# Scatter of both expert layers as row tiles: each product contracts the 64 rows of its batch half

## The chip, the core and the metric

The kernel runs on one core of a Trainium2 chip. A core has five engines that run their own instruction streams and meet at semaphores: PE (TensorE, matrix products into PSUM), DVE (VectorE), ACT (ScalarE), POOL (GpSimd) and SP (SyncE, which issues most transfers here), and 16 DMA engines. The metric is the time of one execution on the device in microseconds (us); less is better.

## What is computed

The input `x` has shape (8, 32, 64, 64): batch, channels, height, width. Four layers are added to it in turn: a spectral convolution (2D Fourier transform, complex product, back), an expert layer on the 4096 tokens of each image, a convolution that sweeps over the image in four directions, row after row, and the same kind of expert layer with other weights. Each layer's input is normalized first. What matters here is the end of an expert layer:

```python
topv = vals.transpose(0, 2, 1)          # the 8 largest gate weights of each expert, over all tokens
topi = idx.transpose(0, 2, 1)           # and which tokens they belong to
...
out = jnp.einsum('ebh,eho->ebo', h, weight2)
out = out.transpose(1, 0, 2)
weighted = jnp.einsum('beo,bke->bkeo', out, topv).reshape(Bn, K * E, O)
outputs = jnp.zeros((Bn, Sn, O), dtype=x.dtype)
outputs = outputs.at[jnp.arange(Bn)[:, None], flat_idx].add(weighted)
```

Each of 16 experts has chosen 8 tokens of each image, and its output vector of 32 channels, times the token's weight, is added to these tokens.

## The kernel before

The image stands in SBUF as 128 rows (4 images x 32 channels) by two halves (images 0 to 3 and 4 to 7: the batch halves `bh`) of 4096 tokens. The scatter is written as a matrix product. `E` has a row for each pair of image and expert (8 x 16 = 128, so rows 0 to 63 belong to batch half 0 and rows 64 to 127 to half 1) and a column for each token; it holds the chosen weights and zero elsewhere. `espread` holds the expert outputs, in 8 blocks of 32 columns, one for each image, and a block is zero in the rows of all other images. The product of 4 blocks (128 columns) with 512 columns of `E` gives the 128 x 512 sums that have to be added to one stretch of 512 tokens of one batch half. So there are 16 products in a layer: 8 stretches (`ch`) for each of 2 halves (`bh`). All values are fp32, and one such product shows in the trace as two passes, each with its own weight load.

**PE** (line 726 on): product `k` goes to PSUM bank `4 + k % 4` and counts up `s_sc`. From product 4 on it waits until the bank is free: for `s_ad`, the count of adds, to reach product k-4's. In layer 0 products 0 to 7 are the stretches of batch half 0 and products 8 to 15 those of half 1; in layer 1 the two halves of a stretch follow each other.

**DVE** waits for `s_sc`, adds the bank to the image in place and counts up `s_ad`: in layer 0 in `add_experts` (line 957) to `RC`, where bank `k` belongs to region `k` of 512 columns, in layer 1 at line 1132 to `RA`.

**Behind layer 0** stands the normalization for the convolution (`norm_tokens(1)`). On PE, `centre_group(1, g)` multiplies 1024 columns of `RC` (regions 2g and 2g+1) with a centring matrix into banks 2(g % 4) and the next. Groups 0 and 1 are woven into the scatter: they are issued behind products 5 and 9 (`FED`). ACT squares a group (line 801) and takes the root of the sums (line 783), DVE sums the squares (`total`, line 934), inverts the root and multiplies (`norm`, lines 941 and 950); then `turn_rows` on PE and copies on ACT (line 790). DVE's own order around the scatter is written out by hand: adds 0 to 5, `total(0)`, adds 6 to 9, `norm(0)`, `total(1)`, adds 10 to 15, `norm(1)`, `total(2)`, and so on. Groups 2 to 7 wait for all 16 adds.

**Behind layer 1** stands only the output: SP waits for two adds at a time (line 379) and issues a store of 512 KB (line 380), eight in all.

Of the kernel before, what the change touches and what calls it, by code (L numbers as in the profile page):

```python
# [10 lines left out]
BL, BH = P // C, B * C // P  # L11
# [7 lines left out]
BANK = 512  # L19
NW = 4  # L20
WRUN = W // NW
MO = P // 2
# [19 lines left out]
def build_kernel(nc, x_in, dft, wspec, conv_w, conv_b, gate_w, gate_b, w1, w2, b2, own, out):  # L42
# [5 lines left out]
    with ExitStack() as ctx:  # L48
        def sb(name, shape, dt=F32):
            return ctx.enter_context(nc.sbuf_tensor(name, shape, dt))  # L50

        def sem(name):
            return ctx.enter_context(nc.semaphore(name))
# [3 lines left out]
        RC, RD = RCD[:, 0:NF], RCD[:, NF:2 * NF]  # L57
        RE = sb("RE", [P, 3 * WCOLS])
        PS = ctx.enter_context(nc.psum_tensor("PS", [P, 8, BANK], F32))
# [21 lines left out]
        espread = sb("espread", [P, B, C])  # L81
# [32 lines left out]
        s_sc, s_ad = sem("scatter_full"), sem("scatter_added")  # L114
# [12 lines left out]
        def blk(region, n):  # L127

            return region[:, n * P:(n + 1) * P]
# [17 lines left out]
        L2, E = RD[:, 0:TOK], RD[:, TOK:2 * TOK]  # L147
# [91 lines left out]
        def ln_slot(g):  # L239

            return banks(2 * (g % 4), 2)
# [189 lines left out]
        def _(pe):  # L431
# [26 lines left out]
            def centre_group(ln, g):  # L458

                if ln == 0:  # L460
                    pe.wait_ge(s_x[g], 16)
                else:
                    pe.wait_ge(s_ad, 2 * g + 2 if g < 2 else 16)
                if g >= 4:
                    pe.wait_ge(s_fd, 8 * ln + g - 3)
                for n in range(8):
                    if ln == 0:
                        m = pe.matmul(blk(ln_slot(g), n), blk(RA, 8 * g + n), centre, start=True, stop=True)  # L468
                    else:
                        first = 1024 * g + BANK * (n // Q)  # L470
                        src = RC[:, first + n % Q:first + BANK:Q]
                        for o in range(0, P, OC):
                            m = pe.matmul(blk(ln_slot(g), n)[o:o + OC], src[:, o:o + OC], centre, start=True, stop=True)  # L473
                m.then_inc(s_cen, 1)

            def norm_tokens(ln, follow):

                def follower(g):
                    pe.wait_ge(s_nrm, 8 * ln + g + 1)
                    follow(g).then_inc(s_ff, 1)  # L480

                if ln == 1:
                    follower(0)
                for g in range(2 * ln, 4):
                    centre_group(ln, g)
                for g in range(ln, 8):
                    follower(g)
                    if 1 <= g < 5:
                        centre_group(ln, g + 3)
# [145 lines left out]
            def experts(l):  # L635
# [8 lines left out]
                for g in range(8):  # L644
# [7 lines left out]
                    for n in range(8):  # L652
                        t, bh = 8 * (g // 2) + n, g % 2
                        src = blk(RC, bh * NT + t) if l == 0 else blk(RA, 8 * g + n)
                        for a in range(2):
                            rows = slice(MO * a, MO * (a + 1))
# [52 lines left out]
                for e in range(NE):  # L709
                    for a in range(2):  # L710
                        units = slice(MO * a, MO * (a + 1))
                        m = pe.matmul(PS[units, 6, B * e:B * e + B], w1_sb[:, e, units], pooled[:, :, e],
                                      start=True, stop=True)
# [11 lines left out]

                pe.wait_ge(s_os, l + 1)
                for k in range(16):
                    if k >= 4:
                        pe.wait_ge(s_ad, 16 * l + k - 3)
                    if l == 0:  # L730
                        bh, ch = divmod(k, 8)
                    else:
                        ch, bh = divmod(k, 2)
                    rhs = E[:, ch * BANK:(ch + 1) * BANK]
                    pe.matmul(PS[:, 4 + k % 4, :], espread[:, BL * bh:BL * bh + BL, :].rearrange("p b o -> p (b o)"), rhs,  # L735
                              start=True, stop=True).then_inc(s_sc, 1)
                    if l == 0 and k in FED:
                        centre_group(1, FED.index(k))

            experts(0)  # L740


# [14 lines left out]
            for s in range(4):  # L757
# [12 lines left out]
                for r in range(1, H):  # L770
                    step(r // Q, r % Q)

            experts(1)


# [148 lines left out]
        def _(dve):  # L924
# [6 lines left out]
            def norm_tokens(ln):  # L931
                def total(g):
                    dve.wait_ge(s_sq, LNS[ln] + g + 1)
                    dve.tensor_reduce(sums[:, 32 * g:32 * g + 32],  # L934
                                      square[:, g % 2, 0:1024].rearrange("p (a c) -> p a c", c=C), AX_X,
                                      ALU.add).then_inc(s_sum, 1)

                def norm(g):
                    r = rstd[:, 32 * g:32 * g + 32]
                    dve.wait_ge(s_std, LN0[ln] + g + 1)  # L940
                    dve.reciprocal(r, std[:, 32 * g:32 * g + 32]).then_inc(s_rec, 1)
                    dve.wait_ge(s_rec, LN0[ln] + g + 1)
                    if ln == 0:
                        m = dve.tensor_tensor(RD[:, 1024 * g:1024 * g + 1024].rearrange("p (a c) -> p a c", c=C),
                                              ln_slot(g).rearrange("p (a c) -> p a c", c=C),
                                              r.unsqueeze(2).to_broadcast([P, 32, C]), ALU.mult)
                    else:
                        for hb in range(2):
                            k = slice(BANK * hb, BANK * (hb + 1))
                            m = dve.tensor_tensor(  # L950
                                RA[:, 1024 * g:1024 * g + 1024][:, k].rearrange("p (b j c) -> p j b c", b=BL, j=Q),
                                ln_slot(g)[:, k].rearrange("p (j b c) -> p j b c", b=BL, j=Q),
                                r[:, 16 * hb:16 * hb + 16].rearrange("p (j b) -> p j b", b=BL).unsqueeze(3)
                                .to_broadcast([P, Q, BL, C]), ALU.mult)
                    m.then_inc(s_nrm, 1)

                def add_experts(first, last):

                    for k in range(first, last):
                        x2 = RC[:, BANK * k:BANK * (k + 1)]  # L960
                        dve.wait_ge(s_sc, k + 1)
                        dve.tensor_tensor(x2, PS[:, 4 + k % 4, :], x2, ALU.add).then_inc(s_ad, 1)

                if ln == 0:
                    total(0)
                    total(1)
                    norm(0)
                    total(2)
                    norm(1)
                    total(3)  # L970
                    norm(2)
                else:
                    add_experts(0, FED[0] + 1)
                    total(0)
                    add_experts(FED[0] + 1, FED[1] + 1)
                    norm(0)
                    total(1)
                    add_experts(FED[1] + 1, 16)
                    norm(1)
                    total(2)  # L980
                    total(3)
                    norm(2)
                for g in range(3, 8):
                    if g < 7:
                        total(g + 1)
                    norm(g)
# [9 lines left out]
            for a in range(2):  # L996
                rows = slice(MO * a, MO * (a + 1))
# [24 lines left out]
            for a in range(2):  # L1022
                rows = slice(MO * a, MO * (a + 1))
# [217 lines left out]
```

## Time and profile before

| | us |
|---|---|
| median of 3 runs | 577.56 |
| the runs | 576.42 to 582.18 |
| the profiled execution | 579.15 |
| its span, from first to last instruction | 577.3 |
| PE busy in the span | 516.2 (89%) |
| DVE, ACT, POOL busy | 323.8, 275.8, 113.3 |
| share of L735 (PE) in the chain that ended last | 5% |

A row of the profile names line, engine, operation and tiles (output<-inputs), then shape and type, then how often (x) and its time. PE stands for the matrix passes, PEld for weight loads. L735 is line 735 of the code. The chain of waits follows the work that ended last, back from the end; a row of it is one stretch of that chain. `RCD` is the tensor of which `RC` and `RD` are the halves, and `RE`, `RA`, `RB` are other large buffers.

### The profile page before, as it was taken

Reading aid. Unit: us, or ns where it says so; the run is one execution under the profiler, and the core shown is the slowest. Engines: PE = TensorE matmul, PEld = TensorE weight load, DVE = VectorE, ACT = ScalarE, POOL = GpSimd, SP = SyncE. Lnnn points to the kernel's source line nnn. Section 1 sums busy time; section 2 is a strip of 40 time slices with the busy share of each in tenths; the row PEclk is TensorE's granted clock in tenths of the full one; section 3 lists DMA queues with packets and bytes.
Section 4 is the critical chain, followed back from the end, with each engine's and each line's share of the span. In section 5 each row is a group of like instructions: output and inputs, shape, how many; then the busy total and the mean of one; then the engine's idle time right before and its main releaser. Section 6 shows DMA issues by size and latency. Waiting matters only on the chain.

```text
span 577.3 us, 25417 instructions
## 1 busy us (share of the span) xinstructions
PE 516.2 (89%) x11282; PEld 462.0 (80%) x11282; DVE 323.8 (56%) x767; ACT 275.8 (48%) x782; POOL 113.3 (20%) x240
## 2 busy tenths in 40 slices
PE   8878999768857999969999999889999999756997
PEld 8878998668747975859999888778899999756973
DVE  2757565833459537754544554445555445669626
ACT  3546554435577102654444444434446777748100
POOL 4000000000161000003333333643331033451000
PEclk9999999989996979988999999979999999976979
DMA  9940990051000000000000033410000244500007
GB/s 351 373 147 2 328 373 36 1 219 76 5 3 1 2 20 2 3 0 3 4 5 3 4 79 76 115 35 4 4 4 3 45 81 82 99 1 1 2 2 291
DMA packets 50259, 41.69 MB, mean 72 GB/s; under 512 B 44998, under 2 KB 45126, under 8 KB 48934
## 3 DMA queue, kind: packets, MB, share of 16 engines
q1 hardware_dynamic: 49304, 38.51, 20.8%
q8 instruction: 90, 1.47, 1.2%
q0 software_dynamic: 704, 1.18, 0.9%
q10 hardware_dynamic: 144, 0.39, 0.2%
q14 instruction: 17, 0.14, 0.1%
HBM read 27.49 MB, written 4.19 MB: 55 GB/s over the span
## 4 chain that ended last, share of the span: by engine, by line
PE 79%; DVE 8%; ACT 6%; POOL 4%; issue 3%; DMA 0%; SPq 0%; POOLq 0%; ACTq 0%; DVEq 0%
PE PS L766 40%; PE PS L550 6%; PE PS L494 5%; PE PS L735 5%; PE PS L591 3%; PE PS L532 3%; PE PS L685 3%; PE PS L473 2%; POOL RE L394 2%; PE PS L436 2%; POOL RCD L397 2%; PE PS L503 2%; DVE sums L1052 1%; PE PS L454 1%; PE PS L468 1%
## 5 line engine op out<-in xcount | busy, mean ns | idle before, releaser
L766 PE MATMUL PS<-RE,conv_sb 128*64 128x64 f32 x6048 | 231.2, 230 | 4.4 <-DVE RE L1151 4.0
L766 PEld LDWEIGHTS PS<-RE,conv_sb 128*64 128x64 f32 x6048 | 210.3, 139 | 25.4 <-DVE RE L1151 4.7
L901 ACT COPY PS<-convb_sb 128x64 f32<-128x64 f32 x504 | 108.2, 215 | 113.0 <-DVE RE L1163 102.6
L1163 DVE SCALAR_TENSOR_TENSOR RE<-PS,RCD 128x64 f32<-128x64 f32 x252 | 56.5, 224 | 58.3 <-PE PS L766 50.0
L406 POOL COPY RCD<-RE 128x128 f32<-128x128 f32 x126 | 37.1, 294 | 156.7 <-DVE RE L1163 156.6
L1163 DVE SCALAR_TENSOR_TENSOR RE<-PS,RE 128x64 f32<-128x64 f32 x126 | 32.6, 259 | 28.4 <-PE PS L766 21.0
L1163 DVE SCALAR_TENSOR_TENSOR RE<-PS,RB 128x64 f32<-128x64 f32 x126 | 28.3, 224 | 28.2 <-PE PS L766 28.2
L494 PE MATMUL PS<-warm 128*128 128x128 bf16 x418 | 35.6, 261 | 3.9 <-DVE warm L929 1.4
L494 PEld LDWEIGHTS PS<-warm 128*128 128x128 bf16 x418 | 32.6, 120 | 5.1 <-ACT RB L879 1.6
L394 POOL TENSOR_TENSOR RE<-RA 128x1024 f32<-128x1024 f32 x3 | 5.7, 1892 | 149.5 <-ACT RA L872 149.5
L550 PE MATMUL PS<-RE,RB 128*64 128x64 f32 x1024 | 32.2, 223 | 1.6 <-DVE RA L991 1.4
L550 PEld LDWEIGHTS PS<-RE,RB 128*64 128x64 f32 x1024 | 30.9, 138 | 2.8 <-issue 2.0
L934 DVE TENSOR_REDUCE sums<-RE 128x32 f32<-128x1024 f32 x16 | 19.4, 1218 | 23.7 <-ACT RE L801 23.7
L1052 DVE TENSOR_REDUCE sums<-RE 128x32 f32<-128x1024 f32 x16 | 19.2, 1201 | 20.7 <-POOL RE L394 17.0
L735 PE MATMUL PS<-RCD,espread 128*128 128x512 f32 x64 | 29.6, 616 | 0.0
L801 ACT ACTIVATE RE<-PS 128x1024 f32<-128x1024 f32 x16 | 16.2, 1022 | 24.1 <-PE PS L473 21.0
L1008 DVE COPY RB<-PS 32x1024 f32<-32x1024 f32 x16 | 19.4, 1214 | 14.7 <-PE PS L532 14.5
L406 POOL COPY RB<-RE 128x128 f32<-128x128 f32 x63 | 18.5, 294 | 40.9 <-DVE RE L1163 40.9
L790 ACT COPY RCD<-PS 128x256 f32<-128x256 f32 (+1 forms) x40 | 17.6, 510 | 15.1 <-PE PS L503 7.7
L591 PE MATMUL PS<-dft_sb,RB 128*128 128x128 f32 x128 | 17.1, 294 | 7.9 <-ACT RE L843 7.6
L735 PEld LDWEIGHTS PS<-RCD,espread 128*128 128x128 f32 x64 | 12.5, 201 | 14.3 <-issue 13.8
L591 PEld LDWEIGHTS PS<-dft_sb,RB 128*128 128x128 f32 x128 | 16.0, 205 | 8.7 <-issue 8.3
(117 smaller groups left out, 691.9 us busy)
## 6 DMA issues: line engine op xcount, KB each, us to landing
RE<-wspec SPq DMA_DIRECT2D x8, 2048.0 KB, 8.7
RA<-x_in SPq DMA_DIRECT2D x8, 512.0 KB, 7.4
RCD<-x_in SPq DMA_DIRECT2D x1, 4096.0 KB, 12.3
out<-RA SPq DMA_DIRECT2D x8, 512.0 KB, 2.7
RCD<-RB SPq DMA_DIRECT2D x58, 64.0 KB, 2.6
RE<-RCD SPq DMA_DIRECT2D x32, 80.0 KB, 2.6
conv_sb<-conv_w SPq DMA_DIRECT2D x1, 768.0 KB, 20.1
w_sb<-w SPq DMA_DIRECT2D x2, 264.0 KB
```

The lines of the kernel that those rows point to most:

```text
L406: pool.tensor_copy(o, i).then_inc(s_arc, 1)
L494: pe.matmul(PS[:, bank, 0:P], warm[:, :], warm[:, :], start=True, stop=True)
L550: m = pe.matmul(o[:, x % 2, y], XB[:, c % 2, 2 * KYC * x + 2 * y + a].rearrange("p r q b -> p (r q b)"), WR[:, c % 3, a, x, y, :], start=T ...
L591: m = pe.matmul(blk(dft_h_slot(g), n), blk(RB, KY * (g % 2) + 8 * (g // 2) + n), inv_h, start=True, stop=True)
L735: pe.matmul(PS[:, 4 + k % 4, :], espread[:, BL * bh:BL * bh + BL, :].rearrange("p b o -> p (b o)"), rhs, start=True, stop=True).then_inc(s ...
L766: m = pe.matmul(conv_bank(s, u, c)[o:o + OC], conv_sb[:, s, d, o:o + OC], prev, start=False, stop=(d == 2), skip_group_check=True)
L790: m = act.copy(o, i)
L901: act.copy(banks_of, convb_sb[:, s:s + 1].unsqueeze(2).to_broadcast([P, c1 - c0, n])).then_inc(s_seed, 1)
L934: dve.tensor_reduce(sums[:, 32 * g:32 * g + 32], square[:, g % 2, 0:1024].rearrange("p (a c) -> p a c", c=C), AX_X, ALU.add).then_inc(s_su ...
L1008: m = dve.tensor_copy(o, i)
L1052: dve.tensor_reduce(sums[:, 32 * g:32 * g + 32], square[:, g % 2, 0:1024].rearrange("p (a c) -> p a c", c=C), AX_X, ALU.add).then_inc(s_su ...
L1163: dve.scalar_tensor_tensor(out=state[:, state_slot(s, u), b0:b1, 1:1 + HO], in0=conv_bank(s, u, c), scalar=0.0, in1=row_at(SRC[s], s, q, u ...
```

## The change

Every product now takes only the 64 rows of its own batch half, of `espread` and of `E` alike; the other 64 rows of `espread` were zero there. In both layers products 2j and 2j+1 are the two batch halves of the same 512-token stretch j, so they use different rows of the array and neighbouring banks. The wait for free banks is taken by the even product for both. In layer 0 the order of the stretches is new, so `add_experts` computes the region, and the first two centre groups wait for other counts: group 0 for 3 adds in place of 2 (products 0 and 2 hold its regions), group 1 for 7 in place of 4 (products 4 and 6).

```diff
@@ centre_group
-                    pe.wait_ge(s_ad, 2 * g + 2 if g < 2 else 16)
+                    pe.wait_ge(s_ad, 4 * g + 3 if g < 2 else 16)
@@ experts, on PE
                 pe.wait_ge(s_os, l + 1)
                 for k in range(16):
-                    if k >= 4:
-                        pe.wait_ge(s_ad, 16 * l + k - 3)
-                    if l == 0:
-                        bh, ch = divmod(k, 8)
-                    else:
-                        ch, bh = divmod(k, 2)
-                    rhs = E[:, ch * BANK:(ch + 1) * BANK]
-                    pe.matmul(PS[:, 4 + k % 4, :], espread[:, BL * bh:BL * bh + BL, :].rearrange("p b o -> p (b o)"), rhs,
-                              start=True, stop=True).then_inc(s_sc, 1)
+                    if k >= 4 and k % 2 == 0:
+                        pe.wait_ge(s_ad, 16 * l + k - 2)
+                    ch, bh = divmod(k, 2)
+                    rows = slice(MO * bh, MO * (bh + 1))
+                    pe.matmul(PS[:, 4 + k % 4, :], espread[rows, BL * bh:BL * bh + BL, :].rearrange("p b o -> p (b o)"),
+                              E[rows, ch * BANK:(ch + 1) * BANK], start=True, stop=True).then_inc(s_sc, 1)
                     if l == 0 and k in FED:
                         centre_group(1, FED.index(k))
@@ add_experts, on DVE
-                        x2 = RC[:, BANK * k:BANK * (k + 1)]
+                        region = 8 * (k % 2) + k // 2
+                        x2 = RC[:, BANK * region:BANK * (region + 1)]
```

The order of instructions on every engine stays; what moves is where PE waits. This is PE in layer 0 from the last warming products to centre group 0 (L473): first before, then after, a line number lower by three (`scatter_added` is `s_ad`, `experts_spread` is `s_os`).

```order
-L735 MATMUL PS<-RCD,espread 128x512 [waits experts_spread]
-L735 MATMUL PS<-RCD,espread 128x512 x3
-L735 MATMUL PS<-RCD,espread 128x512 [waits scatter_added] x2
+L732 MATMUL PS<-RCD,espread 128x512 [waits experts_spread]
+L732 MATMUL PS<-RCD,espread 128x512 x3
+L732 MATMUL PS<-RCD,espread 128x512 [waits scatter_added]
+L732 MATMUL PS<-RCD,espread 128x512
 L473 MATMUL PS<-dft_sb,RCD 64x128 [waits scatter_added]
```

Products 4 and 5 each waited; now product 4 waits for both and product 5 follows without a wait. The same goes for the pairs behind the centre groups. This is PE at the end of the program, layer 1's scatter, before:

```order
L735 MATMUL PS<-RCD,espread 128x512 [waits experts_spread]
L735 MATMUL PS<-RCD,espread 128x512 x3
L735 MATMUL PS<-RCD,espread 128x512 [waits scatter_added] x12
L48 UNCONDITIONAL_BRANCH
```

There every product from the fifth on waited for an add of its own; after the change every second one does, in six pairs like that of layer 0.

## Rows read from the trace of the kernel before

**Rows 1.** The span, and all instructions of L735: duration in ns, least, median, most.

```profile
core 0 of [0], span 577.3 us
L735 PEld LDWEIGHTS PS<-RCD,espread x64: 186/190/337, 211.1 to 572.4; 128*128 128x128 f32 x64
L735 PE MATMUL PS<-RCD,espread x64: 592/592/1167, 211.2 to 572.8; 128*128 128x512 f32 x64
```

**Rows 2.** The chain of waits in order of time: start, us, engine, tile, line, count.

```profile
135.07 1.16 PE PS L454 x64
136.23 0.64 PE PS L436 x16
...
211.44 5.57 PE PS L735 x12
...
231.10 4.06 PE PS L473 x64
...
558.88 14.53 PE PS L735 x32
573.43 0.69 DVE RA L1136
```

**Rows 3.** Timeline of layer 0's scatter: start, us, engine, line, operation [idle before, releaser].

```profile
212.76 0.69 DVE L962 TENSOR_TENSOR RCD<-PS,RCD 128x512 f32<-128x512 f32 x1 [1.97 <-PE PS L735]
...
216.94 2.19 PE L473 MATMUL PS<-dft_sb,RCD 128*64 128x128 f32 x32
...
219.18 1.02 ACT L801 ACTIVATE RE<-PS 128x1024 f32<-128x1024 f32 x1 [12.58 <-PE PS L473]
...
220.24 1.22 DVE L934 TENSOR_REDUCE sums<-RE 128x32 f32<-128x1024 f32 x1 [2.49 <-ACT RE L801]
...
221.37 2.48 DVE L962 TENSOR_TENSOR RCD<-PS,RCD 128x512 f32<-128x512 f32 x4
...
222.69 2.19 PE L473 MATMUL PS<-dft_sb,RCD 128*64 128x128 f32 x32
223.76 0.34 DVE L941 RECIPROCAL rstd<-std 128x32 f32<-128x32 f32 x1
224.14 1.29 DVE L950 TENSOR_TENSOR RA<-PS,rstd 128x512 f32<-128x512 f32 x2
...
225.98 1.22 DVE L934 TENSOR_REDUCE sums<-RE 128x32 f32<-128x1024 f32 x1 [0.55 <-ACT RE L801]
...
227.12 3.84 DVE L962 TENSOR_TENSOR RCD<-PS,RCD 128x512 f32<-128x512 f32 x6
...
231.03 1.16 PEld L473 LDWEIGHTS PS<-dft_sb,RCD 128*64 128x64 f32 x18 [0.17 <-DVE RCD L962]
```

**Rows 4.** Busy time by stretch (us): PE, PEld, DVE, ACT, POOL, PE clock, DMA share, GB/s.

```profile
133.50:151.00 17.50, 14.97 (x647) 13.50 (x642) 9.26 (x8) 8.50 (x9) 0.00 (x0) 1.00 0.02 5
211.20:212.05 0.85, 0.85 (x4) 0.48 (x2) 0.00 (x0) 0.00 (x0) 0.00 (x0) 0.50 0.00 0
558.60:560.20 1.60, 1.60 (x5) 0.85 (x4) 0.00 (x0) 0.00 (x0) 0.00 (x0) 0.50 0.00 0
```

**Rows 5.** Timeline of layer 1's scatter.

```profile
560.55 0.69 DVE L1136 TENSOR_TENSOR RA<-PS,RA 128x512 f32<-128x512 f32 x1 [2.33 <-PE PS L735]
...
561.41 0.69 DVE L1136 TENSOR_TENSOR RA<-PS,RA 128x512 f32<-128x512 f32 x1 [0.17 <-PE PS L735]
...
562.13 12.39 SPq L380 DMA_DIRECT2D out<-RA  x8
```

**Rows 6.** Stretches of the stores: ahead of the first, inside it, behind the last.

```profile
562.50:563.00 0.50, 0.50 (x3) 0.26 (x2) 0.46 (x1) 0.00 (x0) 0.00 (x0) 1.00 0.00 0
563.50:564.00 0.50, 0.50 (x3) 0.24 (x2) 0.33 (x2) 0.00 (x0) 0.00 (x0) 1.00 1.01 385
576.50:577.30 0.80, 0.00 (x0) 0.00 (x0) 0.00 (x0) 0.00 (x0) 0.00 (x0) 0.98 0.00 0
```

## The prediction

> **What bounds the kernel now.** I read the page first, then the chain of waits in order of time, then the timeline of the two stretches that the diff touches, then windows for the TensorE clock and the DMA engines. PE is busy through most of the span, but the scatter (L735) is a small part of it: its 64 passes (32 products, two passes each) [rows 1] stand in two places. In the chain, layer 0's scatter and the two centre groups woven into it begin at 211.44 and the two centre groups behind it at 231.10; layer 1's scatter runs from 558.88 for 14.53 us, and behind it stand one add and the last store [rows 2]. So of 577.3 us some 34 can move at all.
>
> In both places PE sets the pace. In layer 1 the adds of 0.69 us begin 0.86 us apart, as the products come, and DVE idles between them [rows 5]. 0.86 us is two passes of 0.43. DVE can do better: the four adds at 221.37 had their products waiting and took 2.48 us in all, which, with 0.69 for one, is (2.48 - 0.69) / 3 = 0.60 us from one start to the next [rows 3].
>
> **The change part by part.** One: a product of 128 rows becomes one of 64, and both batch halves of a stretch follow each other, on different rows of the array and into different banks. Nothing is removed: 32 products of 512 columns stay. The gain depends on both halves streaming at once. No row shows this for 512 columns, so I bound it. If they stream together, a pair costs what one product costs now, 0.86 us; if not, 1.72. The nearest rows are L454 and L436. L454 makes 64 passes of 64 columns in 1.16 us [rows 2]; at L735's 0.43 us for 512 columns these would take 64 x 0.43 / 8 = 3.44 one by one, so three stream at once, on a quarter of the array each. With only two at once (one row half, both column halves) they would need 1.72. L436 is cut as the new products are (64 rows, all 128 columns of the array): 16 passes in 0.64 us [rows 2] where one by one they need 0.86. I take full overlap, 0.86 a pair, since a 512-column pass has its 0.19 us weight load [rows 1] behind it.
>
> Two: the wait. Before, product k waited for add k-4. Now the even product waits for both adds of the pair before last, and the odd one rides with it. A wait costs: 0.07 us from an add's end (227.12 + 3.84 = 230.96) to the next load (231.03) [rows 3], about 0.1 of the load that no stream covers, 0.43 for the first pass, 0.59 for the whole of the second [rows 1], 0.03 to the add: 1.22 us from add to add. Two banks are being added meanwhile, 1.20 us. So PE and DVE come out almost even: a pair begins 0.60 + 0.69 + 1.22 = 2.51 after the pair before last, 1.26 us a pair against 1.72 now. Queued behind the waiting product on PE are the centre groups in layer 0 and nothing in layer 1.
>
> **Layer 0, step by step** [rows 3]. The first products stream at half clock until 212.05 [rows 4], before and after alike, so add 0 stays at 212.76; adds 1 to 3 follow 0.60 apart. Add 1 ends at 213.36 + 0.69 = 214.05. Products 4 and 5 are streamed by 214.05 + 0.07 + 0.1 + 0.86 = 215.08, and centre group 0 begins at about 215.17 in place of 216.94: 1.77 early. Adds 4 and 5 end at 216.57, ahead of its square. The square (219.18), the sum (220.24) and the adds behind it (221.37) therefore come 1.77 early, so add 6 begins at 219.60. Products 6 to 9 are there by then.
>
> Centre group 1 now waits for add 6, not add 3, since the order of the regions is new. Add 6 ends at 219.60 + 0.69 = 220.29, PE is idle from about 219.1, and the group begins at 220.36 in place of 222.69. This idle costs nothing: its square ends when DVE has done adds 6 to 9 and the norm (223.76 - 1.77, then 0.34 and 1.29), near 223.65. The 0.55 us that DVE now waits ahead of its sum at 225.98 goes too. So that sum comes 2.33 early, add 10 begins near 224.8, products 14 and 15 wait for add 11 and cost DVE 0.1, and add 15 ends at 228.58 in place of 230.96. Centre group 2 waits for all 16 adds before and after, the rest is a chain of PE, ACT and DVE, and layer 0 gives **2.4 us**.
>
> **Layer 1** [rows 5, 6]. Add 0 stays at 560.55. With 1.26 us a pair the last add ends at 560.55 + 7 x 1.26 + 1.29 = 570.7 in place of 573.43 + 0.69 = 574.12, which would be 3.4 us. But each pair of adds releases a store of 512 KB. Today a store moves at 385 GB/s, all 16 DMA engines busy (share 1.01), 1.36 us each, within the 1.72 us of a pair, so each is over before the next. With pairs every 1.26 us the stores queue. The first is issued at 560.55 + 0.60 + 0.69 = 561.84 instead of 562.13, its packets begin 0.9 to 1.0 later (now 563.0), and eight of them take 10.9 us: to 573.7. Now the last packets are over by 576.5, so the end comes **2.7 us** sooner and DMA paces the end. The adds have 0.8 us to spare there.
>
> The Trainium skill, in "TensorEngine Tiling (Array Packing)", section PSUM Bottleneck, says that tiling speeds up TensorE and not the emptying of PSUM, which may become the limit. By that rule the adds would end layer 1: 3.4 us there and 5.8 in all. The stores' share of 1.01 speaks for one limit further on; no row shows eight stores back to back.
>
> **Sum.** 2.4 + 2.7 = 5.1 us off the profiled execution's 579.15, whose span is 577.3: 574.1. The median of the three runs, 577.56, lies 1.6 lower, so I forecast 577.56 - 5.1 = **572.5**. A difference of about 1% (5.8 us) is what a measurement of this kernel can tell from no change, and the runs shown spread from 576.42 to 582.18.
>
> **The rivals.** *The pair overlaps in part.* L454's passes took 1.16 where four at once would take 0.86; at that ratio a pair costs 1.16, 0.3 more. Layer 0 pays it at the first pair, at products 4 and 5 and at 14 and 15 (0.9), layer 1 at the first pair and 0.05 a pair (0.6): 574.0. The Trainium skill, in "TensorE: Matmul & The Clock Gate", Part 3, gives 3.07 times for four row tiles of 512 columns, the same ratio as L454's.
>
> *The adds, not the stores, end layer 1.* For it: stores that follow each other could hide their start. Against it: share 1.01. It gives 571.8.
>
> *The clock falls.* PE would stream 0.86 of every 1.26 us, and stand still for 1.2 us ahead of centre group 1 and near 2 ahead of product 14. The clock was at its lower level as both scatters began [rows 4], after sparse work. If it fell again, the two centre groups behind the scatter, 4.06 us at the full clock [rows 2], would pay up to 4; I take 2.5: 575. Against it: the stretch with 64-row tiles from 133.5 was at 1.00 throughout [rows 4].
>
> *No overlap at all.* The pair takes 1.72, PE sets the pace as now, and the waits bind nowhere: 577.5. The change would then do nothing. Against it: L454 and L436.
>
> *Slower: the halves shut each other out.* If the array had to empty before the other half's rows load and stream, each product would cost 0.1 + 0.43 + 0.59 = 1.12 us in place of 0.86, which is 16 x 0.26 = 4.2 us a layer, 8.4 in all: 586. It decides against the change from a pair of more than 1.72 us on. Against it: L436 alternates between the row halves and gains.
>
> **How the numbers follow.** Forecast 0.60, adds 0.07, part overlap 0.12, clock 0.08, no overlap 0.07, shut out 0.06. The forecast alone would lie within 570.5 to 574.5, the spread of the runs taken in. The range goes from 569.5 (the adds' 571.8, less the 1.1 by which the fastest run lies under the median, less about 1 for a scatter that meets the low clock for less long) to 577.0, just under no change; that leaves out the last two rivals and some of the clock's, under 2 in 10. Faster by over 1% means under 571.8: 0.38 of the forecast, half of the adds', a little of part overlap: 0.28, and I say 0.29. Slower is the last rival: 0.06. Same: 0.65.
>
> **What would show it.** In layer 1: adds in pairs 0.6 apart, pairs 1.26 apart; the last add over near 570.7; DMA share near 1.0 from 563 to the end. In layer 0: centre group 0 some 1.8 us and group 2 some 2.4 us earlier after the scatter's start; PE idle about 1.2 us ahead of centre group 1. Wrong if products of one pair end 0.86 apart (no overlap), if adds spaced further than 1.36 us a pair end layer 1, if DVE's add grows beyond 0.69 while two halves stream, or if the granted clock is below 1.00 between the scatter's second pair and centre group 3.

## The result, and the profile after

Before: median 579.3 us (4 runs, 576.42 to 582.18). Changed: median **570.9 us** (4 runs, 568.43 to 573.18). The ratio is 0.9895 with a 95% interval of 0.9845 to 0.9944, so 6.1 us less, with 3.2 to 9.0 in the interval. It leaves out two runs of before that count as slow (582.18 and 581.04), so the two medians lie further apart than it says. In a second, longer comparison (below) it was 0.9941 (0.9909 to 0.9972), 3.4 us less. The forecast was 5.1 us and 572.5.

The profiled executions differ by more: 577.3 us of span before and 566.6 after. Part of that is not the change's, so the two scatters are read by themselves. First the timeline of layer 0's scatter in the changed kernel (start, us, engine, line, operation, then idle time before and what ended it); the line numbers are lower by two or three.

```profile
206.81 0.48 DVE L1125 SCALAR_TENSOR_TENSOR espread<-PS,rsum,own_sb 128x256 f32<-128x256 f32 x1 [0.85 <-PE PS L722]
207.88 4.58 PE L732 MATMUL PS<-RCD,espread 64*128 64x512 f32 x12
209.99 3.79 DVE L960 TENSOR_TENSOR RCD<-PS,RCD 128x512 f32<-128x512 f32 x6 [2.70 <-PE PS L732]
...
212.39 2.19 PE L473 MATMUL PS<-dft_sb,RCD 128*64 128x128 f32 x32
...
214.51 1.99 PE L732 MATMUL PS<-RCD,espread 64*128 64x512 f32 x8
214.62 1.02 ACT L798 ACTIVATE RE<-PS 128x1024 f32<-128x1024 f32 x1 [11.06 <-PE PS L473]
...
215.68 1.22 DVE L931 TENSOR_REDUCE sums<-RE 128x32 f32<-128x1024 f32 x1 [1.90 <-ACT RE L798]
216.82 2.48 DVE L960 TENSOR_TENSOR RCD<-PS,RCD 128x512 f32<-128x512 f32 x4
...
217.55 2.19 PE L473 MATMUL PS<-dft_sb,RCD 128*64 128x128 f32 x32 [1.06 <-DVE RCD L960]
...
220.84 1.22 DVE L931 TENSOR_REDUCE sums<-RE 128x32 f32<-128x1024 f32 x1
221.98 3.78 DVE L960 TENSOR_TENSOR RCD<-PS,RCD 128x512 f32<-128x512 f32 x6
...
225.81 4.11 PE L473 MATMUL PS<-dft_sb,RCD 128*64 128x128 f32 x64 [0.35 <-DVE RCD L960]
```

Counted from the first add (209.99; before 212.76 [rows 3]), centre group 0 begins after 2.40 us (before 4.18), group 1 after 7.56 (before 9.93), and the last add is over after 221.98 + 3.78 - 209.99 = 15.77 (before 18.20). The first six adds stand in one row of 3.79 us: DVE no longer idles between them. PE idles 1.06 us ahead of group 1.

The row at 214.51 is products 6 to 9, two pairs: eight passes in 1.99 us. First products 6 to 9 in the kernel before, with two of their weight loads, then two of the weight loads in the row at 214.51. The loads are 0.43 us apart in both, one by one before and in twos now:

```profile
219.06 3.70 PE L735 MATMUL PS<-RCD,espread 128*128 128x512 f32 x8
219.60 0.19 PEld L735 LDWEIGHTS PS<-RCD,espread 128*128 128x128 f32 x1 [0.24 <-issue]
220.03 0.19 PEld L735 LDWEIGHTS PS<-RCD,espread 128*128 128x128 f32 x1 [0.24 <-issue]
```

```profile
215.04 0.19 PEld L732 LDWEIGHTS PS<-RCD,espread 64*128 64x128 f32 x2 [0.23 <-issue]
215.47 0.19 PEld L732 LDWEIGHTS PS<-RCD,espread 64*128 64x128 f32 x2 [0.24 <-issue]
```

The lead holds behind the scatter. From the first add to the first product of the convolution (L766, then L763) it is 258.94 - 212.76 = 46.18 us before and 253.91 - 209.99 = 43.92 changed, 2.3 less:

```profile
258.94 5.25 PE L766 MATMUL PS<-RE,conv_sb 128*64 128x64 f32 x108 [0.40 <-ACT PS L901]
```

```profile
253.91 5.36 PE L763 MATMUL PS<-RE,conv_sb 128*64 128x64 f32 x110 [0.40 <-ACT PS L898]
```

Layer 1's scatter:

```profile
549.33 0.48 DVE L1125 SCALAR_TENSOR_TENSOR espread<-PS,rsum,own_sb 128x256 f32<-128x256 f32 x1 [0.60 <-PE PS L722]
...
552.33 10.00 DVE L1134 TENSOR_TENSOR RA<-PS,RA 128x512 f32<-128x512 f32 x16 [2.51 <-PE PS L732]
553.64 9.08 SPq L380 DMA_DIRECT2D out<-RA  x8
```

The sixteen adds take 10.0 us in place of 13.57. The chain of waits (start, us, engine, tile, line, count) now changes sides with every pair, PE and DVE about even, where before it was 14.53 us of PE [rows 2]; it ends with the last add, so the stores behind that show in the windows further down and not here:

```profile
553.67 1.18 PE PS L732 x4
554.85 1.28 DVE RA L1134 x2
556.17 1.18 PE PS L732 x4
557.35 1.28 DVE RA L1134 x2
```

Windows (busy time of PE, PEld, DVE, ACT, POOL, then the granted clock of PE, the DMA share and GB/s): the start of layer 0's scatter and the rest of it, then the stores.

```profile
207.88:210.65 2.77, 2.77 (x9) 1.18 (x8) 0.66 (x2) 0.00 (x0) 0.00 (x0) 0.50 0.00 0
210.65:225.80 15.15, 11.99 (x100) 6.83 (x96) 13.20 (x22) 4.27 (x7) 0.00 (x0) 1.00 0.01 2
...
554.50:565.50 11.00, 5.94 (x22) 1.50 (x20) 7.76 (x13) 0.00 (x0) 0.00 (x0) 1.00 1.01 376
565.90:566.60 0.70, 0.00 (x0) 0.00 (x0) 0.00 (x0) 0.00 (x0) 0.00 (x0) 0.50 0.00 0
```

The DMA engines are full (1.01) from the first store to the end, where one store had been over before the next [rows 6]. From layer 1's first add to the end of the span: 14.27 us, before 16.75.

So the two scatters give 2.4 and 2.5 us from their first add on. The rest of the 10.7 us lies elsewhere, cut at the end of `espread` and of the last add: 3.5 ahead of layer 0's scatter, 3.2 between the two, and in each layer from `espread` to the first add something given back (0.7 and 0.2), which the experiments come to.

### The profile page after: what moved, and what is told of

It is laid out like the page before. It is cut to its first block, busy times and chain, and to the rows that moved or that the text cites. A ratio compares the mean times of both kernels' runs of the same rounds, so it can differ in the third digit from the quotient of the medians.

```text
span 566.6 us, 25417 instructions
## 1 busy us (share of the span) xinstructions
PE 498.5 (88%) x11282; PEld 450.4 (79%) x11282; DVE 321.6 (57%) x767; ACT 275.7 (49%) x782; POOL 115.1 (20%) x240
## 4 chain that ended last, share of the span: by engine, by line
PE 73%; DVE 13%; ACT 6%; POOL 4%; issue 2%; DMA 0%; DVEq 0%; SPq 0%; POOLq 0%; ACTq 0%
PE PS L763 41%; PE PS L550 6%; PE PS L494 4%; PE PS L532 3%; PE PS L591 3%; PE PS L685 3%; POOL RCD L397 2%; POOL RE L394 2%; PE PS L436 2%; PE PS L473 2%; PE PS L732 2%; PE PS L503 2%; DVE sums L931 2%; DVE sums L1050 2%; PE PS L454 1%
## 5 line engine op out<-in xcount | busy, mean ns | idle before, releaser
L763 PE MATMUL PS<-RE,conv_sb 128*64 128x64 f32 x6048 | 231.3, 231 | 4.5 <-DVE RE L1149 4.1
L763 PEld LDWEIGHTS PS<-RE,conv_sb 128*64 128x64 f32 x6048 | 212.7, 139 | 23.0 <-DVE RE L1149 4.8
L494 PE MATMUL PS<-warm 128*128 128x128 bf16 x418 | 31.1, 241 | 3.9 <-DVE warm L926 1.4
L494 PEld LDWEIGHTS PS<-warm 128*128 128x128 bf16 x418 | 28.4, 109 | 4.9 <-ACT RCD L876 1.6
L591 PE MATMUL PS<-dft_sb,RB 128*128 128x128 f32 x128 | 15.7, 279 | 7.9 <-ACT RE L840 7.6
L732 PE MATMUL PS<-RCD,espread 64*128 64x512 f32 x64 | 19.1, 699 | 2.8 <-DVE RCD L960 1.7
L591 PEld LDWEIGHTS PS<-dft_sb,RB 128*128 128x128 f32 x128 | 14.7, 192 | 8.6 <-issue 8.2
L659 PE MATMUL PS<-proj,RA 64*64 64x96 f32 x512 | 14.1, 273 | 8.0 <-DVE RA L343 4.4
```

Source lines behind the costliest of these rows:

```text
L494: pe.matmul(PS[:, bank, 0:P], warm[:, :], warm[:, :], start=True, stop=True)
L591: m = pe.matmul(blk(dft_h_slot(g), n), blk(RB, KY * (g % 2) + 8 * (g // 2) + n), inv_h, start=True, stop=True)
L732: pe.matmul(PS[:, 4 + k % 4, :], espread[rows, BL * bh:BL * bh + BL, :].rearrange("p b o -> p (b o)"), E[rows, ch * BANK:(ch + 1) * BANK], ...
L763: m = pe.matmul(conv_bank(s, u, c)[o:o + OC], conv_sb[:, s, d, o:o + OC], prev, start=False, stop=(d == 2), skip_group_check=True)
```

## The experiments

**How much is the change's: both kernels again.** Nothing edited.

> The changed kernel again, nothing edited, timed in more rounds. Theory A (the two scatters give about 5 us, the rest of the 10.7 us between the two profiled spans is the TensorE clock's lower level met for longer or shorter): from the first add to the end of the last add of layer 0 again 15.8 us (before 18.2), from layer 1's first add to the end of the span again 14.3 us (before 16.75), each within 0.2; the stretch between the two scatters (last add of layer 0 to the end of espread in layer 1, 327.3 before and 324.1 after) may come out anywhere from 323 to 329; the ratio to before near 0.991. Theory B (the change does more than the scatters): that stretch between stays at 324, and the ratio lies near 0.985.

> The kernel before again, nothing edited, for a second trace. Theory A (the stretches without the change differ from run to run with the clock): 18.2 us and 16.75 us in the two scatter stretches again, within 0.2 each, while the stretch between the scatters may come out from 323 to 329 in place of 327.3, and goes with the time spent at the lower clock: about half of any difference in it. Theory B: it stays at 327.3 within 0.5.

Measured: 572.84 us (12 runs) against 577.31 (17 runs), ratio 0.9941 (0.9909 to 0.9972); the second trace of before is one run of 578.02. The scatter stretches repeat: changed 15.93 and 14.22 us, before 18.20 and 16.74. The stretch between the scatters does not belong to either kernel. Its windows, for before, for changed, and for two kernels of the experiments below, the one with 128 rows back and the one with half stores:

```profile
230.96:558.22 327.26, 302.63 (x7410) 276.00 (x7409) 178.12 (x584) 168.85 (x651) 93.73 (x225) 0.95 0.15 29
```

```profile
225.76:549.81 324.05, 299.69 (x7408) 275.94 (x7409) 177.47 (x584) 168.59 (x651) 95.56 (x225) 0.96 0.15 29
```

```profile
232.96:555.80 322.84, 297.84 (x7410) 262.23 (x7409) 178.27 (x585) 168.91 (x651) 93.92 (x225) 0.97 0.15 29
```

```profile
227.99:550.81 322.82, 298.21 (x7408) 262.57 (x7409) 178.25 (x584) 168.67 (x651) 94.15 (x225) 0.97 0.15 29
```

In these four the length goes with the granted clock, 0.95, 0.96, 0.97, 0.97, and not with the scatter: the third one has 128-row products and no gain there, and yet is as short as the fourth. Over all eleven traces clock and length go together only roughly (the second trace of "halves in a row", below, has 327.0 us at 0.95 and "its own wait" 325.4 at 0.96, where changed has 324.1 at 0.96), so that the clock is all of it is not shown. The stretch lay between 322.8 and 327.6; before came out at 327.3 and 327.6, changed at 324.1 and 324.8, with the edits below at 322.8 to 327.0. The two traces of each kernel fit theory B as well as A; it is the edited kernels, short with 128 rows (322.8) and long with 64 (326.7 with a store behind each add), that speak for A. The stretch ahead of layer 0's scatter was 210.8 and 209.0 us in before, 207.3 and 210.3 in changed. So the 6.7 of the 10.7 us that lie in these two stretches come and go with the execution.

**128 rows back in each product.**

```diff
-                    rows = slice(MO * bh, MO * (bh + 1))
+                    rows = slice(0, P)
```

> The changed kernel with the 128 rows back in each product; order of the stretches, the waits for pairs and for the centre groups stay as changed. Theory A (the gain is that two row halves stream at once): two products of 128 rows cannot, so a pair takes 1.72 us, the adds come 0.86 apart, and the stretches are those of before: 18.2 us in layer 0 and 16.75 us in layer 1, within 0.4. Theory B (the new order and the waits bring the gain): 15.8 and 14.3 stay.

Measured: 577.09 us (one run). Layer 0 18.41 us, layer 1 16.97. The adds of layer 1 are 0.86 apart again (timeline):

```profile
559.40 0.69 DVE L1134 TENSOR_TENSOR RA<-PS,RA 128x512 f32<-128x512 f32 x1 [0.39 <-PE PS L732]
560.25 0.69 DVE L1134 TENSOR_TENSOR RA<-PS,RA 128x512 f32<-128x512 f32 x1 [0.17 <-PE PS L732]
561.11 0.69 DVE L1134 TENSOR_TENSOR RA<-PS,RA 128x512 f32<-128x512 f32 x1 [0.17 <-PE PS L732]
```

With the order and the waits of the change and without its rows the gain is gone; both stretches are those of before within 0.25 us. That is theory A.

**64 rows, but the halves in a row.** Layer 0 in the order, waits and regions of before, layer 1 as changed.

```diff
-                    pe.wait_ge(s_ad, 4 * g + 3 if g < 2 else 16)
+                    pe.wait_ge(s_ad, 2 * g + 2 if g < 2 else 16)
...
-                    if k >= 4 and k % 2 == 0:
-                        pe.wait_ge(s_ad, 16 * l + k - 2)
-                    ch, bh = divmod(k, 2)
+                    if k >= 4 and (l == 0 or k % 2 == 0):
+                        pe.wait_ge(s_ad, 16 * l + k - (3 if l == 0 else 2))
+                    if l == 0:
+                        bh, ch = divmod(k, 8)
+                    else:
+                        ch, bh = divmod(k, 2)
...
-                        region = 8 * (k % 2) + k // 2
+                        region = k
```

> The changed kernel with layer 0's products back in the order, the waits and the regions of before (all eight of batch half 0, then all eight of half 1), each still of 64 rows; layer 1 stays as changed. Theory A (a product of 64 rows costs what one of 128 rows costs, and only neighbours on different rows stream at once): layer 0 as before, products 0.86 apart and 18.2 us, but for the two in the middle where the half changes; layer 1 14.3. Theory B (a product of 64 rows is cheaper by itself): layer 0 well under 18.2, near 15.8.

Measured: 581.48 us (one run), layer 0 **23.12 us**, layer 1 14.25. Neither theory had that. On PE (timeline, then windows):

```profile
211.70 10.61 PE L735 MATMUL PS<-RCD,espread 64*128 64x512 f32 x12
222.24 3.70 PE L473 MATMUL PS<-dft_sb,RCD 128*64 128x128 f32 x32
225.86 2.63 PE L735 MATMUL PS<-RCD,espread 64*128 64x512 f32 x8
...
230.53 5.45 PE L735 MATMUL PS<-RCD,espread 64*128 64x512 f32 x12
```

```profile
211.70:222.20 10.50, 10.50 (x13) 3.84 (x12) 3.46 (x5) 0.00 (x0) 0.00 (x0) 0.50 0.00 0
222.20:227.18 4.98, 4.98 (x37) 4.11 (x38) 0.84 (x2) 1.18 (x2) 0.00 (x0) 0.50 0.01 3
227.18:237.00 9.82, 9.82 (x60) 5.18 (x58) 9.79 (x16) 2.79 (x4) 0.00 (x0) 1.00 0.00 1
```

PE streams without a pause, and still the clock stays at 0.50 (1.2 GHz) from the first product to 227.18, 15.5 us; the kernel before reached 1.00 (2.4 GHz) 0.8 us after its first product [rows 4]. At the lower clock the first adds come 1.71 us apart, one product each. At the full clock the last six products cost 0.86 each (5.45 for 12 passes), like products of 128 rows [rows 5]. So theory A holds for the price of a product, and the clock is a second cost that was not in it. The clock rose 1.3 us into the row at 225.86, four products of both halves behind centre group 0; which of the two lifted it no run separates.

**The same again, and with four full products ahead.** The second kernel differs from "halves in a row" in one line:

```diff
-                    rows = slice(MO * bh, MO * (bh + 1))
+                    rows = slice(0, P) if l == 0 and k < 4 else slice(MO * bh, MO * (bh + 1))
```

> The kernel with layer 0's products of 64 rows in the order of before, again, to see whether the clock's long stay at its lower level was chance. In the first run of it the clock stayed at 0.50 from the first product for 15.5 us, through ten products one by one and centre group 0, where the kernel before rose 0.8 us after its first product. Theory A (64-row products one at a time do not lift the clock): again at 0.50 through the first six products and the centre group, first add to last add 22 us or more. Theory B (chance): the clock rises within about 4 us of the first product and the stretch is 18.2 to 19.5.

> The same kernel, but with 128 rows in layer 0's first four products; products 4 to 15 keep 64 rows, one after another. Theory A: the four full products lift the clock as in the kernel before, within about 2 us of the first; two 64-row products and a centre group follow, which is too little to bring it down, so the stretch is that of before, 18.2 to 18.5 us, and products of 64 rows take 0.86 us at the full clock. Theory B (64-row products also let the clock fall): the clock is at 0.50 again somewhere before the last add, and the stretch is over 19.5.

Measured, one run of each: the first again 23.12 us, at 0.50 until 228.16, 15.5 us again (583.91). With four full products the clock rose 1.9 us after the first, stayed at 1.00, and the stretch was 17.59 us (572.55). A window of the first, two of the second, then the timeline of the second:

```profile
212.68:228.16 15.48, 15.48 (x49) 7.95 (x50) 4.30 (x7) 1.19 (x2) 0.00 (x0) 0.50 0.01 1
```

```profile
207.54:209.46 1.92, 1.92 (x5) 0.89 (x4) 0.00 (x0) 0.00 (x0) 0.00 (x0) 0.50 0.00 0
209.46:227.18 17.72, 17.32 (x103) 9.20 (x101) 14.01 (x22) 3.97 (x5) 0.00 (x0) 1.00 0.01 1
```

```profile
207.54 6.52 PE L735 MATMUL PS<-RCD,espread 128*128 128x512 f32 x12
...
216.11 1.99 PE L735 MATMUL PS<-RCD,espread 64*128 64x512 f32 x8
...
220.15 3.70 PE L735 MATMUL PS<-RCD,espread 64*128 64x512 f32 x8
```

Both rows of x8 are four products: 220.15 those of one half, one by one, 3.70 us; 216.11 two of either half, 1.99. The second is the likely reason why the stretch is under the 18.2 expected. Both runs give theory A, but for that.

**Half of each store left out.**

```diff
-                sp.dma_start(halves[:, i // 2, i % 2], done[:, i // 2, i % 2]).then_inc(s_out, 16)
+                sp.dma_start(halves[:, i // 2, i % 2, 0:1], done[:, i // 2, i % 2, 0:1]).then_inc(s_out, 16)
```

> The changed kernel with half of each store left out: only batch half 0 of each pair of adds is written to the output, 256 KB in place of 512 KB, so half of the output is missing. Everything ahead of it stays. Theory A (the stores that queue end layer 1): they do not queue any more, and the end follows the last add at the distance of one short store: the adds take 10.0 us as now, and the end comes about 2.5 us behind them, 12.5 us from the first add in place of 14.27. Theory B (the adds and a fixed tail end it): the tail stays near 4.3 less the 0.7 of the shorter last store, 13.6 us.

Measured: 567.73 us (one run). The adds take 9.99 us as ever, the end comes 12.43 us behind the first add (14.27 changed), 2.44 behind the last (4.27). The windows of the stores:

```profile
555.50:565.00 9.50, 6.11 (x24) 1.50 (x20) 7.92 (x13) 0.00 (x0) 0.00 (x0) 0.94 0.58 220
```

At a share of 0.58 nothing queues, and the adds end the layer. Of the 1.8 us some 0.7 is the shorter last store; the rest, 1.1, is the queue; by as much the changed kernel ends further behind its last add than the kernel before (4.27 against 3.19). That is theory A.

**A store behind each add; group 2 waits for 14 adds.**

```diff
-                    pe.wait_ge(s_ad, 4 * g + 3 if g < 2 else 16)
+                    pe.wait_ge(s_ad, (3, 7, 14)[g] if g < 3 else 16)
...
-            for i in range(2 * NW):
+            for i in range(4 * NW):
...
-                sp.wait_ge(s_ad, 16 + 2 * (i + 1))
-                sp.dma_start(halves[:, i // 2, i % 2], done[:, i // 2, i % 2]).then_inc(s_out, 16)
+                k, h, t = i // 4, i // 2 % 2, i % 2
+                sp.wait_ge(s_ad, 16 + i + 1)
+                sp.dma_start(halves[:, k, h, t], done[:, k, h, t]).then_inc(s_out, 16)
```

> The changed kernel with two further edits. Layer 1: a store of 256 KB behind each add in place of 512 KB behind two, sixteen stores. Layer 0: centre group 2 waits for 14 adds in place of 16 (its banks and regions are free by then). Theory A (the queue of stores ends layer 1 and begins with the first store; layer 0's end hangs on centre group 2): the first store begins one add, 0.6 us, earlier and the end with it: 13.7 us from layer 1's first add in place of 14.27; centre group 2 begins 0.6 us earlier, 15.2 us behind layer 0's first add in place of 15.82. Together 1.2 us, too little for the whole time to tell. Theory B (each store has a cost of its own on the queue): sixteen stores end later than eight, 14.5 us or more.

Measured: 569.19 us (4 runs, 567.72 to 570.28), ratio to before 0.9859 (0.9784 to 0.9934). The end of layer 1 comes 13.47 us behind the first add (0.8 sooner than changed), centre group 2 begins 15.41 us behind layer 0's first (0.4 sooner; not 0.6, since PE is busy with the follower until then). The queue, over 11 us:

```profile
556.50:567.50 11.00, 6.63 (x24) 1.66 (x24) 8.45 (x14) 0.00 (x0) 0.00 (x0) 1.00 1.02 378
```

It is as full as with eight stores, only earlier. That is theory A. By its stretches this version is 1.2 us ahead of the changed kernel, and in layer 0 the lead holds to the first product of the convolution (43.33 us from the first add, 43.92 changed). So it is the best one here; the whole times don't tell the two apart.

**Each product its own wait.**

```diff
-                    if k >= 4 and k % 2 == 0:
-                        pe.wait_ge(s_ad, 16 * l + k - 2)
+                    if k >= 4:
+                        pe.wait_ge(s_ad, 16 * l + k - 3)
```

> The changed kernel with the waits of before: from product 4 on each product waits for the add four ahead of it, the odd ones too, in place of one wait for the pair. Rows, order and regions stay as changed. Theory A (what sets the adds' pace is the way round from an add to the add that its bank allows, 1.2 us plus an add): with a way round of 4 adds in place of two pairs the adds come 0.60 apart all through, 9.7 us from the first add's start to the last add's end in layer 1 in place of 10.0; the end of the span does not move, since the stores end it: 14.25 from the first add. Layer 0 15.5 to 15.8 as now. Theory B (the two halves stream together only where the odd product rides with the even one): products come one by one, 0.86 apart, and layer 1 goes back to 13.6 and 16.75.

Measured: 569.3 us (one run). Layer 1's adds in one row (timeline), and 14.26 us to the end:

```profile
553.24 9.74 DVE L1134 TENSOR_TENSOR RA<-PS,RA 128x512 f32<-128x512 f32 x16 [2.70 <-PE PS L732]
```

Layer 0 15.66 us. The common wait is not what lets the halves overlap; it costs 0.26 us in layer 1, behind which the stores stand anyway. That is theory A.

## Why the prediction was right, step by step

- **The pair streams in the time of one product: right.** At the full clock the passes of both halves start within 0.01 us of each other, and the next two 0.43 later (0.53 behind the first passes of a row); 128-row products in the same places bring nothing. The part-overlap rival is out for 512 columns, no overlap and shut-out too.
- **The way round, 1.26 us a pair: right.** Measured 10.0 us for 16 adds, so (10.0 - 1.29) / 7 = 1.24. With own waits it is DVE's 0.60 an add alone.
- **Layer 0, 2.4 us: right from the first add on.** Group 0 came 1.78 us sooner (forecast 1.77), group 1 2.37 (2.33), the last add's end 2.43 (2.38), 2.27 in the second pair of traces; PE's idle ahead of group 1 was 1.06 (1.2) and cost nothing.
- **"Before and after alike" for the start: wrong.** From the end of `espread` to layer 0's first add it took 1.97 and 2.36 us in before and 2.70 in both traces of changed: 0.3 to 0.7 us given back. The first pass starts 0.59 us behind `espread` in place of 0.45, and the whole first pair and most of the second meet the lower clock (207.88 to 210.65 at 0.50), which in before rose during the first product. Not all of that is the change's: with 128 rows in the first products and the clock low through the first one (four full products ahead) it took 2.51. So about 0.2 us goes with the 64 rows, and whether the change also makes the clock rise later is open: it rose 0.8 to 2.3 us after the first pass with 128 rows and 1.5 to 4.0 with pairs, both layers taken together. Layer 1 gave back about 0.2 (2.33 and 2.37, then 2.51 and 2.56).
- **Layer 1, 2.7 us, the stores end it: right in mechanism, 0.2 too large.** The eight stores took 11.3 us (packets from 554.58 to 565.84), not 10.9 (the forecast's own figures, 576.5 less 573.7, make 2.8). The adds' rival, 3.4 us for layer 1, falls by the 1.1 us that the queue adds. The Trainium skill's rule in "TensorEngine Tiling (Array Packing)", section PSUM Bottleneck, that the emptying of PSUM may become the limit, fits the pace of the adds with own waits (9.74 us in one row) and not the end of the layer.
- **The clock's rival: not in the change, but near it.** In the first trace of changed the clock was at 1.00 from the end of the second pair (210.65) to the end of the scatter, pauses and all; in the second trace it rose 3.8 us after the first pass, DVE idled 0.42 us between its first two pairs, and the stretch was 15.93 us. Products that stream one half alone are where it stayed low; there it had not risen, and it did not fall once up.
- **Sum: right, 0.7 to 1.2 us too large; the total is in part luck.** 2.43 + 2.48, less 0.5 to 1.0 at the two starts, is 3.9 to 4.4 us where 5.1 were forecast; both measured ratios hold it in their intervals. Taken off 577.56 that gives 573.2 to 573.7, and the twelve runs gave 572.84. The median of 570.9 is lower, and the stretches that the change doesn't touch, which the profiled run had short, lie on that side.

## What to carry to other kernels

Products that contract only half of the rows are free to pair: put neighbours on different rows (and, as here, in different banks; no run varied the banks) and the pair costs one product. Then look for what paces the stretch next, twice over; here it was the adds with PE in one place and the output queue in the other, and of the 6.9 us a layer that pairing takes off PE (8 x 0.86) 2.4 and 2.5 were left. Where two profiles differ by more than the stretches that were changed, read the granted clock of the rest before the change is given credit for it.

## What the hardware did that was not expected

**Half the rows, one product at a time, left the clock low.** Two traces, the same both times: 15.5 us of unbroken streaming at 0.50 (six such products, centre group 0 and a part of the next four), where 128 rows in the same order were at 1.00 after 0.8 and 1.6 us in the two traces of before. With pairs of halves the clock rose 1.6 to 3.8 us after their first pass, in five traces. Once up, the clock stayed up over 3.70 and 5.45 us of single halves.

**Products on other rows overtake.** In the kernel with the halves in a row, products 6 and 7 (half 0) stand ahead of 8 and 9 (half 1), and the four took 2.63 us, half of it at the lower clock. At the full clock, with four full products ahead, they took 1.99 as a row of x8, where four of one half take 3.70, and their passes start in twos 0.01 us apart. So 8 streamed beside 6 and not behind 7. A count of finished products (`s_sc`) then need not say which ones are finished; here add 6 began at 218.42, behind the end of all four (218.10). The Trainium skill, in "TensorE: Matmul & The Clock Gate", Part 3, has matmuls in strict program order, start and end; this trace differs, and the measurement decides.

**Cutting the rows has an entry price.** In layer 0 the first 64-row pass came 0.59 us behind `espread` in seven traces, the first 128-row pass 0.45 in four.
